# Transposing by DMA instead of on TensorE, with the DMA lists of SP and ACT reordered, in a fused cross-attention and quantized FFN kernel

## The chip, the cores and the metric

The kernel runs on one core of one Trainium2 chip. The metric is the device time of one execution in microseconds (us). A core has five engines with instruction lists of their own: TensorE (PE, matmuls and transposes by matmul), VectorE (DVE), ScalarE (ACT), GpSimd (POOL) and SyncE (SP, which here only issues DMAs). ACT issues DMAs too; SP and ACT have one DMA queue each, and both queues are served by the same 16 DMA engines. Each list runs strictly in order, and a semaphore wait in it holds everything behind it.

## What is computed

x and ctx are (16, 64, 256) float32: 16 batches, 64 rows, 256 columns. The attention has 8 heads of 8 rows; q is the layernorm of x, and ctx is both key and value.

```python
qk  = einsum('bhdq,bhdl->bhql', q, k) * 8**-0.5
ret = einsum('bhql,bhdl->bhdq', softmax(qk), v)
x   = x + gamma * ret
# the FFN, on a = layernorm(x); every bit_linear rounds its input rows to
# integers in -128..127 (scale: row maximum) and its weights to -1, 0, 1
h   = silu(bit_linear(a, w_gate)) * bit_linear(a, w_up)     # 256 -> 1024
h   = rms_norm(h, ln_weight)
out = x + bit_linear(h, w_down)                             # 1024 -> 256
```

## The kernel before

The 1024 rows are T = 8 tiles of 128 partitions (two batches each). A tile has 16 heads (BH), and the heads of all tiles are one stream of 128, numbered n. Time in the program is counted in half steps m: head n is at m = 2n, so a tile is 32 half steps. Every engine's list is written by a loop over m, and a table of numbers says at which m a piece of work stands: `tile_at(m, r)` gives the tile u with m = r + 32u. A larger number puts a piece later in that engine's list. All engines use the same m, so the numbers show who stands ahead of whom.

Each head has two score matmul pairs. A (psA, L433) gives scores with queries on partitions, from which DVE takes the negated row maximum (mneg, L736). B (psB, L447) gives the scores again, transposed, with the maximum already subtracted: three extra rows of q_stack hold the maxima as three bf16 parts, against rows of ones in k_stack. ACT takes the exponential (probs, L594), and a third matmul group (psO, L463, fp32) sums values and denominators for four heads at a time. B runs LAG = 14 heads behind A.

The maxima get there thus: for each half tile (8 heads) POOL splits them (m_parts), PE transposes them, ACT copies them to mt (L622), and SP moves 12 KB with a DMA (L398) from mt into the three rows of q_stack. This mt DMA stands at m = 20 + 16k. B of the first half of tile t waits for it at m = 29 + 32t.

The stacks: x (normalised, as xhat) and ctx are split into three bf16 parts (q_parts, k_parts), stored to scratch in HBM by six DMAs of 64 KB a tile (L301), and loaded back by six DMAs of 192 KB (L333, L341) into q_stack and k_stack, which have three buffers. SP_STORE = -26 and SP_LOAD = -20 place them: the loads of a tile are at m = 12 modulo 32. At the start SP also loads x and ctx of tiles 2 to 7 in two DMAs of 768 KB, and the three weights (1 MB each) in twelve DMAs spread over m = 12 to 33.

The FFN of a tile stands behind its attention, beside the heads of later tiles. DVE and POOL make the layernorm and its scale, ACT rounds (aq, L642), PE transposes aq in two 128x128 blocks (L520), ACT evicts to aT as bf16 (L648); PE multiplies by the gate and up weights in two halves (L535), ACT, DVE and POOL make h and weigh it (hw), DVE takes its row maximum (h_max, L834), ACT rounds (hq, L676), PE transposes eight blocks (L555), ACT evicts them to hT (L684), and PE multiplies by the down weight (L565). The weights are rounded once, in tile 1 (POOL L923, DVE L747), transposed by PE in twelve groups of four blocks (L498), and evicted by ACT and DVE in turn (L636, L755). Rounding adds and later subtracts 1.5 x 2^23. For the last tile some of this goes to DVE.

Of the kernel before, what the change touches and what calls it, by code (L numbers as in the profile page):

```python
# [5 lines left out]
ALU = mybir.AluOpType  # L29
# [5 lines left out]
P = 128  # L35
# [49 lines left out]
PE_WB, WB_STEP, WB_LAG = 56, 2, 0  # L85
POOL_INIT, DVE_STATS = 16, 14
# [28 lines left out]
def build(nc, x, ctx_in, gamma, w_gate, w_up, w_down, ln_weight, out):  # L115
# [7 lines left out]
    with ExitStack() as ctx:  # L123
# [48 lines left out]
        aq = sb("aq", [P, L])  # L172
        aT = sb("aT", [P, KC, P], BF16)
# [16 lines left out]
        hq = sb("hq", [P, HID])  # L190
        hT = sb("hT", [P, IC, P], BF16)
# [11 lines left out]
        wgT = sb("wgT", [P, 2, KC, HID], BF16)  # L203
        wdT = sb("wdT", [P, IC, L], BF16)
# [26 lines left out]
        s_stack = [sem(f"stack_loaded{i}") for i in range(NBUF)]  # L231
        s_a = sem("a_scores")
# [24 lines left out]
        s_aT = sem("aT_ready")  # L257
# [14 lines left out]
        s_hT = sem("hT_ready")  # L272
# [70 lines left out]

        def load_ones(eng, t):

            eng.dma_start(k_stack[STACK:STACK_M, t],
                          one_rows[:, :].unsqueeze(1).to_broadcast([PARTS, BH, L])).then_inc(s_ones[t], DMA)

        @block.sync
        def _(sp):  # L350
            def load_w(k, j):

                wide = w_sb[:, k, :].rearrange("p (c n) -> p c n", c=4)
                if k < 2:
                    rows = (w_gate, w_up)[k].rearrange("(j c p) n -> j p c n", c=2, p=P)[j]
                    sp.dma_start(wide[:, j, :].rearrange("p (c n) -> p c n", c=2), rows).then_inc(s_w[k], DMA)
                else:
                    half = slice(512 * (j % 2), 512 * (j % 2 + 1))
                    sp.dma_start(wide[:, j, :], w_down[P * (j // 2):P * (j // 2 + 1), half]).then_inc(s_w[k], DMA)

# [6 lines left out]
            load_q(sp, 0)  # L367
            sp.wait_ge(s_rows, 1)
            load_ones(sp, 0)
            sp.dma_start(x_sb[:, 2:T, :], x_rows[2:T].rearrange("g p l -> p g l")).then_inc(s_x[2], DMA)  # L370
            sp.dma_start(c_sb[:, 2:T, :], ctx_rows[2:T].rearrange("g p l -> p g l")).then_inc(s_c[2], DMA)
            for m in range(2 * FIRST, 2 * LAST):
                n = m // 2
                t = tile_at(m, SP_STORE)
# [19 lines left out]
                k = half_at(m, ACT_M)  # L394
                if k is not None:
                    t, half = divmod(k, 2)
                    sp.wait_ge(s_mtsb, k + 1)
# [610 lines left out]
```

## Time and profile before

| | us |
|---|---|
| median of 3 runs | 244.86 (244.29 to 246.13) |
| span of the profiled execution | 248.6 |
| PE busy | 178.4 (72%) |
| DVE busy | 151.6 (61%) |
| ACT busy | 140.9 (57%) |
| POOL busy | 107.3 (43%) |

The profile is of one execution; it lists busy time of each engine, the granted clock of TensorE in slices, and for every instruction what its engine waited for before it. Matmuls overlap, so a busy PE is not PE at its peak. A wait counts only where it stands on the path that sets the end.

### The profile page before, as it was taken

Reading aid. Unit: us, or ns where it says so; the run is one execution under the profiler, and the core shown is the slowest. Engines: PE = TensorE matmul, PEld = TensorE weight load, DVE = VectorE, ACT = ScalarE, POOL = GpSimd, SP = SyncE. Lnnn points to the kernel's source line nnn. Section 1 sums busy time; section 2 is a strip of 40 time slices with the busy share of each in tenths; the row PEclk is TensorE's granted clock in tenths of the full one; section 3 lists DMA queues with packets and bytes.
Section 4 is the critical chain, followed back from the end, with each engine's and each line's share of the span. In section 5 each row is a group of like instructions: output and inputs, shape, how many; then the busy total and the mean of one; then the engine's idle time right before and its main releaser. Section 6 shows DMA issues by size and latency. Waiting matters only on the chain.

```text
span 248.6 us, 4308 instructions
## 1 busy us (share of the span) xinstructions
PE 178.4 (72%) x1370; PEld 103.8 (42%) x1378; DVE 151.6 (61%) x282; ACT 140.9 (57%) x286; POOL 107.3 (43%) x282
## 2 busy tenths in 40 slices
PE   0006331972988958994999799589979998893793
PEld 0002111540666624662466366245745664441432
DVE  2105840563297974985666989736886769436273
ACT  4110000893466845973568599447856587975432
POOL 3630310406624544734652586436435226626240
PEclk9999999996599997997569999965995699999689
DMA  3599599348201450253026314601540000000000
GB/s 100 139 142 261 126 177 313 115 121 154 63 1 37 118 107 0 56 149 77 1 67 141 75 26 116 135 9 34 142 105 0 5 3 22 7 21 0 22 1 21
DMA packets 15871, 19.95 MB, mean 80 GB/s; under 512 B 2649, under 2 KB 14057, under 8 KB 14697
## 3 DMA queue, kind: packets, MB, share of 16 engines
q1 hardware_dynamic: 15321, 18.89, 31.8%
q10 hardware_dynamic: 528, 0.79, 1.4%
q8 instruction: 11, 0.18, 0.3%
q14 instruction: 11, 0.09, 0.1%
HBM read 15.20 MB, written 4.19 MB: 78 GB/s over the span
## 4 chain that ended last, share of the span: by engine, by line
PE 33%; DMA 14%; DVE 7%; issue 6%; ACT 6%; POOL 4%; SPq 3%; POOLq 0%; ACTq 0%; DVEq 0%
DMA q_stack<-mt 13%; PE psO L463 9%; PE psB L447 7%; PE psA L433 6%; PE psG L565 2%; PE psG L505 2%; ACT probs L594 2%; PE psG L555 2%; POOL hw L325 2%; DVE mneg L736 1%; SPq L333 1%; ACT o_sb L629 1%; SPq L341 1%; DVE wgT L755 1%; DVE w_sb L747 1%
## 5 line engine op out<-in xcount | busy, mean ns | idle before, releaser
L736 DVE TENSOR_REDUCE mneg<-psA 128x2 f32<-128x512 f32 x128 | 82.7, 680 | 46.5 <-PE psA L433 46.4
L594 ACT ACTIVATE probs<-psB 128x512 f32<-128x512 f32 x128 | 74.0, 597 | 39.8 <-PE psB L447 39.7
L433 PE MATMUL psA<-k_stack,q_stack 72*128 72x256 bf16 x256 | 57.9, 319 | 23.1 <-DMA q_stack<-q_scratch 20.7
L447 PE MATMUL psB<-q_stack,k_stack 75*128 75x256 bf16 x256 | 55.2, 303 | 23.8 <-DMA q_stack<-mt 22.0
L463 PE MATMUL psO<-probs,vt 128*32 128x256 f32 x512 | 41.6, 451 | 1.0 <-ACT probs L594 1.0
L433 PEld LDWEIGHTS psA<-k_stack,q_stack 72*128 72x128 bf16 x256 | 23.9, 108 | 43.3 <-issue 30.1
L447 PEld LDWEIGHTS psB<-q_stack,k_stack 75*128 75x128 bf16 x256 | 25.7, 108 | 37.2 <-DMA q_stack<-mt 23.8
L325 POOL TENSOR_TENSOR hw<-h,lnw 128x512 f32<-128x512 f32 x15 | 19.1, 1270 | 39.3 <-DVE h L826 28.0
L463 PEld LDWEIGHTS psO<-probs,vt 128*32 128x32 f32 x512 | 14.8, 121 | 16.9 <-issue 9.9
L815 DVE SCALAR_TENSOR_TENSOR gu<-th,psG 128x512 f32<-128x512 f32 x15 | 10.3, 688 | 9.7 <-ACT th L657 9.7
L657 ACT ACTIVATE th<-psG,tscale 128x512 f32<-128x512 f32 x15 | 10.3, 688 | 9.1 <-PE psG L535 9.0
L931 POOL CAST m_parts<-mneg 128x16 bf16<-128x16 f32 x16 | 3.7, 230 | 19.7 <-DVE mneg L736 12.4
L676 ACT ACTIVATE hq<-hw,h_sig 128x1024 f32<-128x1024 f32 (+1 forms) x8 | 8.7, 1091 | 5.3 <-POOL h_sig L984 2.8
L622 ACT ACTIVATE mt<-psU 48x128 bf16<-48x128 bf16 x16 | 4.3, 270 | 12.9 <-PE psU L479 12.9
L826 DVE TENSOR_TENSOR h<-psU,gu 128x512 f32<-128x512 f32 x15 | 10.4, 691 | 0.5
L834 DVE TENSOR_REDUCE h_max<-hw 128x1 f32<-128x1024 f32 x8 | 9.7, 1212 | 1.4 <-POOL hw L325 1.4
L694 ACT ACTIVATE vt<-psU 128x128 f32<-128x128 f32 x16 | 3.7, 298 | 12.0 <-PE psU L473 12.0
L505 PE MATMUL psG<-ident,o_sb 128*128 128x128 f32 x32 | 6.9, 354 | 4.2 <-ACT o_sb L629 3.3
L565 PE MATMUL psG<-wdT,hT 128*128 128x256 bf16 x64 | 9.1, 289 | 0.7 <-DVE hT L850 0.4
L535 PE MATMUL psU<-wgT,aT 128*128 128x512 bf16 x30 | 9.4, 395 | 0.1
L923 POOL TENSOR_SCALAR w_sb<-w_sb,winv 128x2048 f32<-128x2048 f32 x3 | 5.9, 1974 | 7.9 <-DVE whalf L743 7.9
L762 DVE RECIPROCAL rden<-psG 128x32 f32<-128x32 f32 x8 | 2.9, 357 | 9.4 <-PE psG L505 9.4
(129 smaller groups left out, 268.4 us busy)
## 6 DMA issues: line engine op xcount, KB each, us to landing
q_stack<-q_scratch SPq DMA_DIRECT2D x24, 192.0 KB
k_stack<-k_scratch SPq DMA_DIRECT2D x21, 192.0 KB
q_scratch<-q_parts SPq DMA_DIRECT2D x24, 64.0 KB, 2.1
k_scratch<-k_parts SPq DMA_DIRECT2D x21, 64.0 KB, 2.0
w_sb<-in_L_ffn_w_gate_dram SPq DMA_DIRECT2D x4, 256.0 KB, 8.0
w_sb<-in_L_ffn_w_up_dram SPq DMA_DIRECT2D x4, 256.0 KB, 7.5
w_sb<-in_L_ffn_w_down_dram SPq DMA_DIRECT2D x4, 256.0 KB, 4.1
out_dram<-y_sb SPq DMA_DIRECT2D x8, 128.0 KB, 4.2
```

The lines of the kernel that those rows point to most:

```text
L325: eng.tensor_tensor(hw[:, half], h[:, half], lnw[:, half], ALU.mult).then_inc(s_hw, 1)
L433: mm = pe.matmul(psA[n % A_BANKS][:, qt * L:(qt + 1) * L], q_stack[0:STACK, t % NBUF, bh, qt * P:(qt + 1) * P], k_stack[0:STACK, t % NBUF, ...
L447: mm = pe.matmul(psB[b % 2][:, lt * L:(lt + 1) * L], k_stack[:, t % NBUF, bh, lt * P:(lt + 1) * P], q_stack[:, t % NBUF, bh, :], start=Tru ...
L463: mm = pe.matmul(psO[32 * j:32 * (j + 1), half * L:(half + 1) * L], vt[:, t % 2, lt, half * GROUP + j, par, :], probs[:, (GROUP * g + j) % ...
L505: mm = pe.transpose(banks[BANK_OTR][:, k * P:(k + 1) * P], o_sb[:, k * P:(k + 1) * P], ident[:, :])
L565: mm = pe.matmul(banks[BANK_DOWN][:, 0:L], hT[:, ic, :], wdT[:, ic, :], start=(ic == 0), stop=(ic == IC - 1))
L594: act.activation(probs[:, b % RING, :], psB[b % 2][:, :], ACT.Exp, scale=SCALE).then_inc(s_exp, 1)
L657: act.activation(th[:, c, :], gate_up(u, c)[0][:, :], ACT.Tanh, scale=tscale[:, 0:1]).then_inc(s_th, 1)
L736: dve.tensor_reduce(mneg[:, k % MBUF, QT * (bh % HALF):QT * (bh % HALF + 1)], psA[n % A_BANKS][:, :].rearrange("p (q l) -> p q l", q=QT), ...
L815: dve.scalar_tensor_tensor(out=gu[:, c, :], in0=th[:, c, :], scalar=1.0, in1=gate_up(u, c)[0][:, :], op0=ALU.add, op1=ALU.mult).then_inc(s ...
L826: dve.tensor_tensor(h[:, c * 512:(c + 1) * 512], gate_up(u, c)[1][:, :], gu[:, c, :], ALU.mult).then_inc(s_h, 1)
L834: dve.tensor_reduce(h_max[:, :], hw[:, :], AX.X, ALU.max, apply_absolute_value=True).then_inc(s_hmax, 1)
```

## The change

1. SP's list: the mt DMA is written first at each m; the stores go to m = 21 modulo 32 (SP_STORE = -43) and the loads to m = 5 modulo 32 (SP_LOAD = -27). The making of the parts on ACT and POOL moves some 16 half steps ahead.
2. The stacks of tile 0 are loaded in halves of eight heads, and head 0 waits only for the first half. x and ctx of tiles 2 to 7, and each weight in one DMA, are issued by ACT, after all of tile 0's stacks landed.
3. aq is converted to bf16 by POOL (aq_b), hq likewise (hq_b), the rounded weights by DVE (wq_b), and `dma_start_transpose` on SP's queue writes aT, hT and the transposed weights. PE keeps these transposes for the last tile alone; the evictions go with them.
4. Gate, up, h, hq and down move some 5 to 9 half steps later in all lists.

Cut to what matters (the table of numbers in two lines, since its effect is shown below):

```diff
-SP_STORE, SP_LOAD, SP_OUT = -26, -20, 119
+SP_STORE, SP_LOAD, SP_AT, SP_HT, SP_OUT = -43, -27, 82, 115, 128
...
+        def load_first(eng, k, half):
+            heads = slice(half * HALF, (half + 1) * HALF)
+            done = (s_first, s_stack[0])[half]
+            for c in range(PARTS):
+                rows = slice(REP * c, REP * (c + 1))
+                if k == 0:
+                    eng.dma_start(k_stack[rows, 0, heads, :].rearrange("p b l -> p (b l)"),
+                                  k_scratch[0, :, c, heads].rearrange("d b l -> d (b l)").unsqueeze(1)
+                                  .to_broadcast([DH, PARTS, HALF * L])).then_inc(done, DMA)
+                else:
+                    eng.dma_start(q_stack[rows, 0, heads, :].rearrange("p b l -> p (b l)"),
+                                  q_scratch[0, :, :, heads].rearrange("d c b l -> (d c) (b l)")).then_inc(done, DMA)
...
+                k, off = divmod(m - SP_WT, WQ_STEP)
+                if off == 0 and 0 <= k < 3:
+                    sp.wait_ge(s_wb, k + 1)
+                    dst = wgT[:, k].rearrange("p i k q -> p (i k) q") if k < 2 else wdT[:, :, :, :].rearrange("p h i q -> p (h i) q")
+                    sp.dma_start_transpose(dst, wq_b[:, k, :]).then_inc(s_wT, DMA)
+                u = tile_at(m, SP_AT)
+                if u is not None and u < T - 1:
+                    sp.wait_ge(s_aqb, u + 1)
+                    if u:
+                        sp.wait_ge(s_u, 2 * u)
+                    sp.dma_start_transpose(aT[:, :, :], aq_b[:, :]).then_inc(s_aTd, DMA)
+                u = tile_at(m, SP_HT)
+                if u is not None and u < T - 1:
+                    sp.wait_ge(s_hqb, u + 1)
+                    if u:
+                        sp.wait_ge(s_y, u)
+                    sp.dma_start_transpose(hT[:, :, :], hq_b[:, :]).then_inc(s_hTd, DMA)
...
+                if m in ACT_BULK:
+                    j = ACT_BULK.index(m)
+                    if j == 0:
+                        act.wait_ge(s_first, 2 * PARTS * DMA)
+                        act.wait_ge(s_stack[0], 2 * PARTS * DMA)
+                        act.dma_start(x_sb[:, 2:T, :], x_rows[2:T].rearrange("g p l -> p g l")).then_inc(s_x[2], DMA)
...
+                    dve.wait_ge(s_wq, k + 1)
+                    dve.tensor_scalar(wq_b[:, k, :], w_sb[:, k, :], ROUND, None, ALU.subtract).then_inc(s_wb, 1)
...
+                u = tile_at(m, POOL_HB)
+                if u is not None and u < T - 1:
+                    pool.wait_ge(s_hq, u + 1)
+                    if u:
+                        pool.wait_ge(s_hTd, DMA * u)
+                    pool.tensor_scalar(hq_b[:, :], hq[:, :], -ROUND, 0.0, ALU.add, ALU.add).then_inc(s_hqb, 1)
```

SP's list in a middle tile, before. x2 means that the row stands twice; L398 is the mt DMA, L403 the store of a finished tile.

```order
L398 DMA q_stack<-mt 3x16x128 [waits max_rows_copied]
L301 DMA k_scratch<-k_parts 16x8x256 [waits first_part]
...
L301 DMA q_scratch<-q_parts 16x8x256 [waits third_part]
L333 DMA k_stack<-k_scratch 24x1x4096 [waits k_part0_stored0,b_scores]
...
L341 DMA q_stack<-q_scratch 24x4096 x2
L398 DMA q_stack<-mt 3x16x128 [waits max_rows_copied]
L403 DMA out_dram<-y_sb 128x256 [waits out_made]
```

The same place after the change:

```order
L363 DMA q_stack<-mt 3x16x128 [waits max_rows_copied]
L314 DMA k_stack<-k_scratch 24x1x4096 [waits k_part0_stored0,b_scores]
...
L322 DMA q_stack<-q_scratch 24x4096 x2
L394 DMA_TRANSPOSE aT<-aq_b 128x2x128 [waits up_done,a_as_bf16]
L400 DMA_TRANSPOSE hT<-hq_b 128x8x128 [waits down_done,h_as_bf16]
L363 DMA q_stack<-mt 3x16x128 [waits max_rows_copied]
L282 DMA k_scratch<-k_parts 16x8x256 [waits first_part]
```

The loads stood close ahead of the first half's mt; now they stand close behind the other half's, and two transposing DMAs stand between them and the first half's mt.

PE's list in a middle tile after the change, where the transposed data are wanted (L555 is down, L526 gate and up, L450 B):

```order
L555 MATMUL psG<-wdT,hT 128x256 [waits hT_landed,x1_made]
L555 MATMUL psG<-wdT,hT 128x256 x7
L450 MATMUL psB<-q_stack,k_stack 128x256 [waits exps]
L450 MATMUL psB<-q_stack,k_stack 128x256
L526 MATMUL psG<-wgT,aT 128x512 [waits out_made,aT_landed]
L526 MATMUL psG<-wgT,aT 128x512
L526 MATMUL psU<-wgT,aT 128x512 [waits max_rows_copied]
L526 MATMUL psU<-wgT,aT 128x512
L436 MATMUL psA<-k_stack,q_stack 128x256 [waits row_max]
L436 MATMUL psA<-k_stack,q_stack 128x256
L450 MATMUL psB<-q_stack,k_stack 128x256 [waits exps,max_rows_loaded0]
```

Down of the tile before (m = 26), gate (27) and B's wait for mt (29) now stand within three half steps.

## Rows read from the trace of the kernel before

**Rows 1.** The page: the granted clock in 40 slices.

```profile
PEclk9999999996599997997569999965995699999689
```

**Rows 2.** Waits: whole run, then about 162.5 and 86 (total, times, longest).

```profile
PE psB L447 <- DMA q_stack<-mt: 22.0, 6, 8.7
...
PE psB L447 <- DMA q_stack<-mt: 3.8, 1, 3.8
...
PE psB L447 <- DMA q_stack<-mt: 3.2, 1, 3.2
```

**Rows 3.** Timeline of SP's queue: start, duration, line, what was issued.

```profile
62.75 14.71 SPq L398 DMA_DIRECT2D q_stack<-mt  x2
...
82.27 2.19 SPq L333 DMA_DIRECT2D k_stack<-k_scratch  x3
...
86.56 14.66 SPq L398 DMA_DIRECT2D q_stack<-mt  x2
...
192.56 11.49 SPq L398 DMA_DIRECT2D q_stack<-mt  x2
```

**Rows 4.** The chain that ended last, about the mt of tile 2.

```profile
86.56 7.27 DMA q_stack<-mt
93.87 0.39 PE psB L447 x2
```

**Rows 5.** Stretches: length, busy of PE, PEld, DVE, ACT, POOL; clock, DMA.

```profile
66.00:86.00 20.00, 18.00 (x166) 13.04 (x164) 16.97 (x31) 13.78 (x30) 7.88 (x23) 0.96 0.15 39
...
140.70:154.70 14.00, 13.26 (x129) 8.69 (x131) 12.41 (x25) 12.53 (x29) 10.10 (x31) 1.00 0.21 56
154.70:162.50 7.80, 4.06 (x35) 1.98 (x34) 5.18 (x9) 3.35 (x6) 3.08 (x3) 1.00 0.59 127
162.50:180.10 17.60, 17.30 (x128) 10.60 (x130) 11.40 (x22) 12.73 (x29) 9.23 (x30) 0.71 0.23 63
...
185.70:203.00 17.30, 17.05 (x127) 10.77 (x128) 11.94 (x24) 11.32 (x23) 7.46 (x27) 0.70 0.01 2
```

**Rows 6.** DMA: 79 to 81 (stores), 85 to 87 (loads), a store's landing.

```profile
q1 hardware_dynamic: 444, 0.20, 39.5%
...
q1 hardware_dynamic: 69, 0.41, 73.6%
...
k_scratch<-k_parts SPq DMA_DIRECT2D x21, 64.0 KB, 2.0
```

**Rows 7.** Groups by line: busy, mean ns of one, idle before.

```profile
L923 POOL TENSOR_SCALAR w_sb<-w_sb,winv 128x2048 f32<-128x2048 f32 x3 | 5.9, 1974 | 7.9 <-DVE whalf L743 7.9
...
L498 PE MATMUL psG<-ident,w_sb 128*128 128x128 f32 x24 | 4.1, 299 | 0.7 <-DVE on L770 0.7
...
L747 DVE TENSOR_SCALAR w_sb<-w_sb 128x2048 f32<-128x2048 f32 x3 | 3.7, 1221 | 1.5 <-POOL w_sb L923 1.5
```

**Rows 8.** Start: timeline of SP, PE and DVE; x's load from the page.

```profile
9.60 1.50 SPq L341 DMA_DIRECT2D q_stack<-q_scratch  x3
...
20.70 4.37 PE L433 MATMUL psA<-k_stack,q_stack 72*128 72x256 bf16 x16 [20.70 <-DMA q_stack<-q_scratch]
...
25.52 2.04 DVE L725 BATCH_NORM_STATS2 stats<-x_sb 128x6 f32<-128x256 f32 x6
...
32.64 0.78 SPq L398 DMA_DIRECT2D q_stack<-mt  x1
...
42.59 0.61 PE L447 MATMUL psB<-q_stack,k_stack 75*128 75x256 bf16 x2 [8.70 <-DMA q_stack<-mt]
...
x_sb<-in_x_dram SPq DMA_DIRECT2D x1, 768.0 KB, 11.1
```

**Rows 9.** Timeline of the end: h_inv and hq of tile 6, then tile 7.

```profile
227.96 0.32 POOL L979 TENSOR_SCALAR h_inv<-h_max,cr 128x1 f32<-128x1 f32 x1 [0.18 <-POOL cr L974]
...
229.23 1.15 ACT L676 ACTIVATE hq<-hw,h_sig 128x1024 f32<-128x1024 f32 x1 [2.62 <-POOL h_sig L984]
...
231.46 0.42 DVE L804 TENSOR_REDUCE a_max<-xn 128x1 f32<-128x256 f32 x1
...
235.04 0.63 PE L535 MATMUL psG<-wgT,aT 128*128 128x512 bf16 x1 [0.88 <-ACT aT L648]
```

More of the change, by code:

```diff
@@ L172, in build @@
         aq = sb("aq", [P, L])
+        aq_b = sb("aq_b", [P, L], BF16)
         aT = sb("aT", [P, KC, P], BF16)
@@ L350, in _ @@
         def _(sp):
[L351 to L359, printed above, removed]
             for t in range(2):
@@ L393, in _ @@
                     sp.dma_start(gam[:, :], gamma.partition_broadcast(P)).then_inc(s_lnw, DMA)
[L394 to L397, printed above, removed]
-                    sp.dma_start(q_stack[STACK:STACK_M, t % NBUF, half * HALF:(half + 1) * HALF, :]
-                                 .rearrange("c b (q l) -> c (b q) l", q=QT), mt[:, k % 2, :]).then_inc(s_mrow[half], DMA)
+                k, off = divmod(m - SP_WT, WQ_STEP)
[15 more added lines that the diff above has]
+                    sp.dma_start_transpose(hT[:, :, :], hq_b[:, :]).then_inc(s_hTd, DMA)
                 u = tile_at(m, SP_OUT)
@@ L420, in keep_clock @@
                 for _ in range(count):
-                    pe.matmul(psB[0][:, :], aT[:, 0, :], wgT[:, 0, 0, 0:512], start=True, stop=True)
+                    pe.matmul(psB[0][:, :], aT[:, 0, :], wgT[:, 0, 0:4, 0, :], start=True, stop=True)
             pe.wait_ge(s_ident, 2)
@@ L427, in _ @@
                     t, i, bh = unit(n)
-                    if i == 0:
+                    if n == 0:
+                        pe.wait_ge(s_first, 2 * PARTS * DMA)
+                    elif i == (0 if t else HALF):
                         pe.wait_ge(s_stack[t % NBUF], 2 * PARTS * DMA * (t // NBUF + 1))
@@ L515, in _ @@
                 u = tile_at(m, PE_ATR)
-                if u is not None:
-                    take(BANK_ATR, s_aT, u + 1)
+                if u == T - 1:
+                    take(BANK_ATR, s_aT, 1)
                     pe.wait_ge(s_aq, u + 1)
@@ L547, in _ @@
                     u = tile_at(m, r)
-                    if u is not None:
-                        last = (u, c) == (T - 1, 0)
-                        pe.wait_ge(*((s_hq, u + 1) if not last else (s_hq_last, 1)))
+                    if u == T - 1:
+                        pe.wait_ge(*((s_hq_last, 1), (s_hq, T))[c])
                         bank = banks[(BANK_HTR0, BANK_HTR1)[c]]
-                        take((BANK_HTR0, BANK_HTR1)[c], *((s_hT, min(2 * u + c + 1, 2 * T - 1)) if not last else (s_hT_last, 1)))
+                        take((BANK_HTR0, BANK_HTR1)[c], (s_hT_last, s_hT)[c], 1)
                         for j in range(4):
@@ L585, in _ @@
             act.wait_ge(s_p3, 2)
-            load_k(act, 0)
+            for c in range(PARTS):
+                act.wait_ge(s_kst[c][0], DMA)
+            load_first(act, 0, 0)
+            load_first(act, 0, 1)
             for m in range(2 * FIRST, 2 * LAST):
```

150 lines of the change are left out of this document (71 added, 79 removed).

## The prediction

> **What bounds the kernel now.** I read the page first, then the waits, then the stretches between them. The page gives a span of 248.6 us for the profiled execution; the median of the plain runs is 244.86 us, 1.5% less, so the sum is made against 248.6 and scaled by 0.985 at the end. Its clock line [rows 1] shows full clock (2.4 GHz) broken by four dips of about 12 us each to near the lower level (1.2 GHz). The waits [rows 2] name one culprit: the B matmuls (psB, L447) wait 22.0 us in six waits for the 12 KB DMA that puts the negated row maxima (mt) into q_stack. The longest, 8.7 us, is at the start; the other five share 13.3 us, and a typical bad one is 3.8 us.
>
> SP's rows [rows 3] show why. The six loads of the next tile's stacks are issued from 82.27 on, and mt only at 86.56, behind them on the same queue; it lands 7.27 us later [rows 4]. From the first load to that landing are 11.6 us; the same distance in the other tiles is near 11.
>
> The stretches [rows 5] give the price. From 140.7 to 162.5, a tile of 21.8 us, the clock was full and PE was busy 13.26 + 4.06 = 17.3 us. Take off the 3.8 us that psB waited and a tile needs 18.0 us. In the stretches from 162.5 and 185.7 the same 128 or so matmuls took 17.30 and 17.05 us at granted clocks of 0.71 and 0.70, against 13.26 at 1.00: each bad tile pays some 4 us for the clock beside the wait, after PE had stood. mt was issued at 86.56 for tile 2 and at about 203.3 for tile 7 [rows 3], so a tile takes 23.3 us now.
>
> **The change, part by part.** *SP's list.* The loads now follow at once behind the mt of one half tile (step 5 of 32), and the next mt is at step 20. B needs mt at step 29: 24 half steps after the loads begin, 13.5 us in a tile of 18 us, against 8.4 us now (82.27 to PE's arrival at 90.7, which is 93.87 [rows 4] less its wait of 3.2 [rows 2]). The loads and mt together took 11.6. Alone this would remove all five waits, and with them the reason for the dips.
>
> But two transposing DMAs, aT and hT, now stand between the loads and mt, in the same queue, with two consumers of their own: down (PE step 26) and gate (step 27). Their price is the open one. Nothing in this trace transposes by DMA. I count in blocks of 128x128 bf16 (32 KB): aT is 2, hT 8, each weight 16. The nearest row by size of piece: in 79 to 81 us, 444 small packets took 39.5% of 16 engines over 2 us, 28 ns each [rows 6]. A block is 128 runs of 256 B, shorter than these packets of some 450 B; I take 26 ns each, which over 16 engines makes **0.21 us**. Below that, a block as cheap as bytes moved by the stack loads (0.41 MB in 2 us while they ran [rows 6]) is 0.16 us. Above it, a block that needs an issue of its own costs like the stack loads' issues, 2.19 us for three, or 0.73 [rows 3]. I take 0.21, the row nearest in shape; 0.16 and 0.73 stay as ends.
>
> At 0.21, aT and hT add 2.1 us to the 11: hT is there 13.1 us after the loads began, down wants it at 21 half steps or 11.8 us, so PE waits about 1.3 us, and gate and mt are then ready. Call it 1 us a tile.
>
> The Trainium skill speaks against the change: VectorE: DVE Perf Modes, The three transpose paths, gives 1309 ns for a 128x128 bf16 block by DMA and 390 ns on TensorE. By it the sum below would end near 333 us. Another page of the Trainium skill, Advanced Engine Details and Errata, X-Bar Transpose (TRN2), has these DMAs nearly as fast as plain ones (350 to 400 GB/s); by that, an estimate of 0.09 us a block, the result would be near 206. No row here shows either.
>
> *Work leaving PE.* aT's and hT's transposes in seven tiles: ten blocks each, like those of the weights near 0.17 us (4.1 us of 24 [rows 7]), less at full clock, about 1.3 us of PE a tile, and three evictions less on ACT. PE is then at 16.0, but DVE is not relieved: it was busy 12.41 + 5.18 = 17.6 us in the tile from 140.7 [rows 5], which this change leaves. So the tile stays at 18.0, now bound by DVE, and 18.0 + 1 = 19.0 against 23.3: five tiles give **21.5 us**. The conversions on POOL (1 us for hq, half of 1974 ns for 2048 columns, and 0.5 for aq [rows 7]) hide under POOL's idle third; without it they would lengthen the chain to hT.
>
> *Weights.* 48 PE transposes of 0.17 us leave: 8 us off the tile of 23.8 us from 62.75 to 86.56 [rows 3, 7]. DVE loses its six evictions and pays three conversions of 2048 columns, near 1.2 us each as its own pass over a weight is [rows 7], some 3.7 for what was 4: no difference. It was busy 16.97 of the 20 us from 66 to 86 [rows 5], so no more than its 3.0 us of idle time can go: **3 us**. The three weight DMAs, 48 blocks or 10 us, have 20 half steps (13 us) before B wants the next mt; covered, barely.
>
> *Start.* A starts at 20.70, 11.1 us after the q loads were issued at 9.60 [rows 8]. With half stacks loaded first, A starts at 14 to 18. But A head 7's maximum waits on DVE for statistics of x of six tiles, and that load is issued later than now: by ACT, after all stacks landed, at about 18. It takes between 4.5 us (0.77 MB at the 200 GB/s of [rows 6]) and the 11.1 it took [rows 8], so it lands at 22.5 to 29. From statistics to issue of mt 7.1 us pass now (25.52 to 32.64) [rows 8]; mt then finds the loads of tile 1 done. B starts at 32 to 39 against 42.59; I take 34, a gain of **8.6 us**. Until 62.75 nothing else moves.
>
> *Tail.* Tile 6 was helped by PE transposes; now its down stands directly ahead of tile 7's gate in PE's list, and ACT's hq of tile 6 ahead of tile 7's aq. Now a_max of tile 7 starts at 231.46, its gate at 235.04 [rows 9], and hq of tile 6 is over before. In the new order DVE takes tile 6's h_max (1.2 us) only after that a_max, then follow POOL's chain 1.3 (227.96 to 229.23), hq 1.15 [rows 9], the conversion 1.0, the DMA 3.7 (a 64 KB store lands in 2.0 [rows 6], and 8 blocks are 1.7), down 1.0: about 9.4 us after a_max where gate now comes after 3.6. **+6 us.**
>
> Sum: 21.5 + 3 + 8.6 - 6 = 27.1; 248.6 - 27.1 = 221.5, by 0.985 **218 us**.
>
> **One number carries the risk.** Let b be the us per block. A tile's stall is 10b - 1, five times; the weights cost 48b less the 10 that fit; the tail 8b. Together the change of the span is -27.1 + 106(b - 0.21). It is zero at b = 0.47.
>
> **Rivals.** *A, slower: the transposes clog SP's queue.* The place is SP's queue between the stack loads and mt; it decides from b = 0.47 on. At b = 0.6 the stall is 5 us a tile, the weights alone hold mt some 19 us, and the time is (248.6 - 27.1 + 41.3) x 0.985 = 259 us. For it: 0.73 as the upper bound; hT would hold mt every tile. Against: the small-packet row. 0.13. The 1309 ns of the Trainium skill (VectorE: DVE Perf Modes) would be a case of this rival.
>
> *B, the wait moves.* b is near 0.3, or the loads end later because the conversions and waits of SP's in-order list hold them. PE stands 2 to 3 us a tile, at hT rather than at mt, and the clock dips stay in some tiles: a tile of 22 instead of 19. 218 + 15 = 233 us, or 228 if only the stands stay (106 x 0.09 above the forecast). For it: all three consumers lie within 3 half steps, and the slack is under 2 us. 0.17.
>
> *C, better than forecast.* b at 0.16 or below and B starting at 32: the stall (5 us) and 2 us of the start go, tiles of 17.7: 218 - 8.5 = 209 us or less. 0.12.
>
> *D, gain and loss meet* (b from 0.44 to 0.49): within 1%, 0.03.
>
> **Numbers.** The forecast case (211 to 225 us) has 0.55. The range is 207 to 234: it leaves out A, D and a thin end of C. A difference of 1% is about what can be told from none. Faster: forecast, B and C, 0.84; within 1%, 0.03; slower, A, 0.13.
>
> **What would show it.** Right: no wait of psB for mt over 1 us after the first; waits of down for hT near 1 us; a granted clock above 0.95 from 80 us on; mt issues 19 us apart per tile; B starting by 36 us; a longer gap between the last psO and the last gate, near 16 us. Wrong: DMA transposes landing over 4 us after issue with an idle queue (A), a tile of 22 with dips (B), x landing after 29 us (the start's gain gone). If the first gate matmul waits long for the weights, the 48 blocks were mispriced.

## The result, and the profile after

The changed kernel takes **319.64 us** (median of 4 runs, 316.89 to 320.8) against 245.5 us of the kernel before, a ratio of 1.301 (95% interval 1.291 to 1.310). The forecast was 218 us, the range 207 to 234. Medians here are of all executions and ratios of the faster ones alone (an execution more than 1.5% above its kernel's fastest is left out of them), and the profile of the kernel before, with its span of 248.6 us, is of an execution some 2 us slower than any of the four behind its median.

The page of the changed kernel, its span, busy times and the granted clock in 40 slices (compare [rows 1]):

```profile
span 315.1 us, 4050 instructions
...
PE 181.0 (57%) x1260; PEld 88.3 (28%) x1260; DVE 156.8 (50%) x279; ACT 129.5 (41%) x259; POOL 142.2 (45%) x296
...
PEclk9999999857599967995799589958995975576579
```

PE has 118 transposes fewer (48 of weights, 14 of aq, 56 of hq) and was busy longer: the clock now dips in nearly every tile, where before it dipped four times. POOL has 35 us more. The waits (total, times, longest), the last for comparison with [rows 2]:

```profile
DVE mneg L730 <- PE psA L436: 90.7, 40, 9.3
...
POOL hw L306 <- DVE h L815: 58.2, 8, 10.3
...
POOL rstd L927 <- DVE mv L780: 31.8, 8, 4.7
...
ACT hq L672 <- POOL h_sig L985: 26.4, 7, 7.8
...
ACT k_parts L605 <- DMA c_sb<-in_ctx_dram: 21.2, 1, 21.2
...
PE psG L555 <- DMA hT<-hq_b: 11.2, 2, 6.1
...
PE psB L450 <- DMA q_stack<-mt: 4.9, 1, 4.9
```

PE's wait for mt is gone but for the first (4.9, where the six took 22.0), as forecast, and hT makes PE wait twice only. What grew are waits of POOL, ACT and DVE for one another. SP's queue in a tile, and the transposes' median time from issue to landing (compare [rows 3]):

```profile
149.93 0.82 SPq L363 DMA_DIRECT2D q_stack<-mt  x1
...
165.32 2.14 SPq L314 DMA_DIRECT2D k_stack<-k_scratch  x3
167.51 1.27 SPq L322 DMA_DIRECT2D q_stack<-q_scratch  x3
177.89 1.22 SPq L394 DMA_TRANSPOSE aT<-aq_b  x1
179.20 1.25 SPq L400 DMA_TRANSPOSE hT<-hq_b  x1
```

```profile
aT<-aq_b SPq DMA_TRANSPOSE x7, 2.4
hT<-hq_b SPq DMA_TRANSPOSE x7, 3.1
...
wgT<-wq_b SPq DMA_TRANSPOSE x2, 4.3
wdT<-wq_b SPq DMA_TRANSPOSE x1, 4.5
```

The DMAs are not slow: 2, 8 and 16 blocks land in 2.4, 3.1 and 4.3 us. But aT is issued 9 us after the loads, since SP stood waiting for aq_b. The whole tile, and two stretches in it (columns as in [rows 5]):

```profile
149.90:180.90 31.00, 19.20 (x156) 9.76 (x154) 17.32 (x30) 14.98 (x33) 16.93 (x35) 0.83 0.28 68
170.00:175.00 5.00, 1.49 (x10) 0.74 (x10) 3.04 (x5) 2.82 (x5) 4.41 (x12) 0.85 0.57 123
175.00:180.90 5.90, 1.17 (x5) 0.53 (x6) 0.00 (x0) 2.02 (x7) 5.48 (x9) 0.50 0.15 32
```

In these 10.9 us PE is busy 2.7 us, DVE not at all in the second half, and POOL 9.9 us. Its list there (start, duration, instruction, and in brackets the idle time before it and what ended that):

```profile
165.56 0.19 POOL L927 TENSOR_SCALAR rstd<-mv 128x1 f32<-128x1 f32 x1 [4.12 <-DVE mv L780]
...
166.36 1.27 POOL L306 TENSOR_TENSOR hw<-h,lnw 128x512 f32<-128x512 f32 x1
...
170.50 0.19 POOL L985 TENSOR_TENSOR h_sig<-h_rec,cr 128x1 f32<-128x1 f32 x1
...
173.18 3.65 POOL L961 TENSOR_SCALAR hq_b<-hq 128x1024 bf16<-128x1024 f32 x1
176.79 1.07 POOL L955 TENSOR_SCALAR aq_b<-aq 128x256 bf16<-128x256 f32 x1
177.86 0.55 POOL L892 TENSOR_SCALAR xhat<-x_sb,rstd,shift 128x256 f32<-128x256 f32 x1
```

15 us without a gap over 0.3 us: POOL first waited 4.12 us for mv with h ready behind it, then came all of h's pieces, then hq_b at 3.65 us (the prediction had 1), then aq_b, then xhat and m_parts. ACT stood 4.89 us for that xhat with exponentials behind it in its list, and PE stood 6.21 us for the exponentials.

**Where the 66.5 us between the two profiled spans are** (by the issue of the first mt of each tile; before, by [rows 3, 8]): the start +5.4 (38.0 against 32.6), tile 0 to 1 -1.8, tile 1 to 2 +0.7, the five tiles to tile 7 +33.9 (30.1 us each against 23.3), from there to the end +28.3 (73.6 against 45.3), which holds most of one more slow tile and the tail.

### The profile page after: what moved, and what is told of

It reads as the page before. It is cut to its first block and busy times, and to the rows that moved or that the text cites. A ratio compares the mean times of both kernels' runs of the same rounds, so it can differ in the third digit from the quotient of the medians.

```text
span 315.1 us, 4050 instructions
## 1 busy us (share of the span) xinstructions
PE 181.0 (57%) x1260; PEld 88.3 (28%) x1260; DVE 156.8 (50%) x279; ACT 129.5 (41%) x259; POOL 142.2 (45%) x296
## 5 line engine op out<-in xcount | busy, mean ns | idle before, releaser
L450 PE MATMUL psB<-q_stack,k_stack 75*128 75x256 bf16 x256 | 59.2, 323 | 41.1 <-ACT probs L587 35.4
L436 PE MATMUL psA<-k_stack,q_stack 72*128 72x256 bf16 x256 | 59.2, 326 | 25.8 <-DMA q_stack<-q_scratch 16.6
L466 PE MATMUL psO<-probs,vt 128*32 128x256 f32 x512 | 46.4, 494 | 0.0
L450 PEld LDWEIGHTS psB<-q_stack,k_stack 75*128 75x128 bf16 x256 | 24.8, 112 | 60.1 <-ACT probs L587 45.1
L961 POOL TENSOR_SCALAR hq_b<-hq 128x1024 bf16<-128x1024 f32 x7 | 25.5, 3648 | 0.6
L847 DVE SCALAR_TENSOR_TENSOR y_sb<-psG,yscale,x 128x256 f32<-128x256 f32 x8 | 3.9, 484 | 32.7 <-PE psG L555 32.7
L482 PE MATMUL psU<-ident_b,m_parts 128*48 128x128 bf16 x16 | 4.3, 266 | 24.4 <-POOL m_parts L923 15.1
L555 PE MATMUL psG<-wdT,hT 128*128 128x256 bf16 x64 | 10.6, 321 | 11.6 <-DMA hT<-hq_b 11.2
L526 PE MATMUL psG<-wgT,aT 128*128 128x512 bf16 x30 | 10.2, 427 | 10.8 <-DVE gu L804 7.6
L927 POOL TENSOR_SCALAR rstd<-mv 128x1 f32<-128x1 f32 x8 | 1.5, 190 | 31.8 <-DVE mv L780 31.8
L605 ACT ACTIVATE k_parts<-c_sb 128x256 bf16<-128x256 f32 x7 | 2.9, 413 | 27.0 <-DMA c_sb<-in_ctx_dram 21.2
L555 PEld LDWEIGHTS psG<-wdT,hT 128*128 128x128 bf16 x64 | 7.2, 115 | 14.5 <-issue 12.0
```

The source lines that it names most:

```text
L436: mm = pe.matmul(psA[n % A_BANKS][:, qt * L:(qt + 1) * L], q_stack[0:STACK, t % NBUF, bh, qt * P:(qt + 1) * P], k_stack[0:STACK, t % NBUF, ...
L450: mm = pe.matmul(psB[b % 2][:, lt * L:(lt + 1) * L], k_stack[:, t % NBUF, bh, lt * P:(lt + 1) * P], q_stack[:, t % NBUF, bh, :], start=Tru ...
L466: mm = pe.matmul(psO[32 * j:32 * (j + 1), half * L:(half + 1) * L], vt[:, t % 2, lt, half * GROUP + j, par, :], probs[:, (GROUP * g + j) % ...
L526: mm = pe.matmul(bank[:, :], aT[:, kc, :], wgT[:, w, 4 * c:4 * (c + 1), kc, :], start=(kc == 0), stop=(kc == KC - 1))
L555: mm = pe.matmul(banks[BANK_DOWN][:, 0:L], hT[:, ic, :], wdT[:, :, ic, :], start=(ic == 0), stop=(ic == IC - 1))
L961: pool.tensor_scalar(hq_b[:, :], hq[:, :], -ROUND, 0.0, ALU.add, ALU.add).then_inc(s_hqb, 1)
```

## The experiments

Two theories to start with. **The ring:** the tile is a ring of dependent work through in-order lists, and the conversions and the late FFN pieces made that ring longer than PE's work. **The queue:** SP's new order or the transposing DMAs in it hold the tile up. Letters of theories are those of each expectation. A short diff shows the main numbers of the table that differ; the matching pieces of the other engines move with them. Differences in us are of medians. Runs whose labels begin with the same letter were measured together; between such groups the kernel before itself moved by some us, so there the difference of two ratios (0.01 is 2.5 us) is the surer one.

### The SP order, and the late places

*x4: the kernel before, with part 1 of the change alone.*

```diff
-ACT_QK1, ACT_QK2 = -31, -25   POOL_XHAT, POOL_QK1, POOL_QK3 = -29, -26, -19   SP_STORE, SP_LOAD = -26, -20
+ACT_QK1, ACT_QK2 = -48, -41   POOL_XHAT, POOL_QK1, POOL_QK3 = -46, -42, -35   SP_STORE, SP_LOAD = -43, -27
+ the mt DMA written first at each m
```

> The kernel before with only the making, storing and loading of the stacks moved ahead and mt first in SP's list; FFN places, PE's transposes and the start are as before. The prediction's term for SP's list: the five waits of psB for mt (13.3 us) and part of the clock dips go, 220 to 235. If the waits only move to another engine: 240 to 247.

Measured 226.33 us, ratio 0.935 (0.925 to 0.944). Its clock line and one tile:

```profile
PEclk9999999999559999999999999999999999999599
105.25:124.06 18.81, 17.48 (x163) 10.75 (x164) 16.53 (x31) 16.20 (x35) 12.23 (x33) 1.00 0.40 98
```

A tile of 18.8 us at full clock with PE busy 17.5: the mechanism of this term of the prediction was right, and this one piece beats both kernels, by 16 us (14 to 18) in the ratio to the kernel before. It is the base for what follows.

*x3: x4 with all FFN places of the change (PE's transposes kept).*

```diff
-PE_G0, PE_G1, PE_HTR0, PE_HTR1, PE_DOWN = 86, 88, 105, 108, 113      POOL_HW0, POOL_HW1, POOL_CR, POOL_H = 97, 100, 100, 101
+PE_G0, PE_G1, PE_HTR0, PE_HTR1, PE_DOWN = 91, 93, 110, 113, 122      POOL_HW0, POOL_HW1, POOL_CR, POOL_H = 100, 104, 105, 107
```

> The kernel before with the changed kernel's places for all pieces and its order of SP's list, but no transposing DMAs, no conversions, and the start as before: PE transposes and ACT evicts as before. Theory L (the places alone cost the time): over 290. Theory P: the loads no longer stand ahead of mt, so it is near the kernel before or better, 230 to 250; the tail is still longer by some 5 us since tile 6's down stands ahead of tile 7's gate.

295.44 us, ratio 1.221 (1.204 to 1.237): **the late places alone, without one transposing DMA, cost 69 us** (Theory L). The queue is out as the main cause.

*y3: x3 with h's pieces ahead of the next tile's rstd on POOL* (HW0, HW1, CR, H = 100, 101, 102, 102; rstd stands at 103; on DVE h_max goes from 105 to 100).

> As x3_late_ffn (no transposing DMAs, PE transposes; 295 us) with the same h pieces put ahead. Theory R: near x4_sp_order_only (226) plus a longer tail, 228 to 245. Rival S: over 270, since hq, transposes and down stay at their late steps.

275.51 us, ratio 1.117 (1.106 to 1.128). POOL's order was 20 us of the 69 (26 by the ratios); 49 stay, which is Rival S.

*z2: x4 with hq, its transposes, down and out late (in the last tile alone its gate part is late too); z3: x4 with gate, tanh and h late* (h's pieces as in y3; hq, its transposes and down 2 steps later).

```diff
z2  -ACT_HQ, PE_HTR0, PE_HTR1, PE_DOWN = 101, 105, 108, 113    +ACT_HQ, PE_HTR0, PE_HTR1, PE_DOWN = 108, 110, 113, 122
z3  -PE_G0, PE_G1, ACT_HQ, PE_DOWN = 86, 88, 101, 113          +PE_G0, PE_G1, ACT_HQ, PE_DOWN = 91, 93, 103, 115
```

> The kernel before with the new SP order (226.3 us by itself) and only the down part late: hq 108, its PE transposes 110 and 113, down and out 122, the gate part at the places of before (86 to 101; in the last tile alone 5 steps later, since its down has to stand behind). With gate and down both late and h's POOL pieces ahead of the next rstd it was 275.5. Theory K, late pieces cost only where gate (step 27, 29) and down (26) stand together in the two shared banks psG and psU, one eviction behind the other: here down 26 stands 2 steps behind G1 (24) and 6 ahead of the O transposes, so little: 226 to 240. Theory L, down's place alone (its bank is handed on to the O transposes, its late end holds back y_sb and h of the next tile): 260 or more.

> The same base with only the gate part late: G0, G1 91 and 93, tanh 91, 92, g*u 93 to 95, h's pieces on POOL 100 to 102, hq 103, transposes 107 and 110, down 115. Theory K as above: gate 27, 29 stand 10 steps behind down (19) and 3 ahead of the O transposes (32): 226 to 240. Theory G, gate's own place costs (its second half at 29 and h*u at 31 stand right ahead of the O transposes at 32, so psG and psU are handed on one behind the other there, and with them the next tile's x1, xn): 260 or more, and the trace then has PE waiting for gu or th of DVE and ACT ahead of its next B.

250.5 us (ratio 1.025, 0.992 to 1.058) and 251.09 us (1.031, 1.022 to 1.041). All theories missed: 24.2 and 24.8 us over x4, and together (y3) 49.2 (by the ratios 22, 24 and 45). The two add up, so a crowd of gate and down in the shared banks (Theory K) does not explain them, and neither place is harmless. One tile of z2, one of y3, one of z3:

```profile
130.00:154.42 24.42, 20.46 (x164) 11.19 (x165) 16.80 (x30) 16.57 (x35) 12.20 (x33) 0.90 0.30 71
111.65:139.62 27.97, 22.08 (x166) 11.76 (x165) 16.81 (x30) 16.53 (x35) 12.27 (x33) 0.87 0.25 63
130.49:152.63 22.14, 18.01 (x165) 10.67 (x164) 16.59 (x31) 15.98 (x35) 12.27 (x33) 1.00 0.33 80
```

DVE, ACT and POOL are as busy as in x4. In z2 and y3 PE does the same work in 3 to 4.6 us more, at a lower clock, and the rest is standing; in z3's tile the clock is full and nearly all of the 3.3 us is standing. No single wait is long: PE's in the tile of z2 are 1.3 us and less. But PE's waits of the whole run of z2 show where they are:

```profile
PE psG L557 <- ACT hq L678: 6.3, 7, 1.2
...
PE psU L522 <- ACT hT L686: 4.9, 7, 1.8
PE psU L557 <- ACT vt L696: 4.3, 5, 1.3
```

With 3.7 us of down's waits for gu these are 19.2 us, where x4 has 1.9 us for hq, 1.7 for vt at this bank, and none of the others: 15.6 of the 23.4 us between the two spans. Three of the four are waits for the piece that empties a shared PSUM bank. In psU (hT and vt, 9.2 us) the transposes of ctx, hq and aq stand at steps 15, 17 and 18 in z2 (hq's at 12 in x4), and in psG (gu) down stands 2 steps behind gate. So the hand-over of banks goes with what down's place costs, and the one at psU is a part that the changed kernel does not have, since its PE transposes neither hq nor aq but in the last tile. In z3 it is mostly waits for hq (9.7 us) and of gate for gu (8.4), where x4 has 1.9 and none. No run took the banks apart.

### The conversions

*x1: the changed kernel, with DVE in POOL's place for aq_b and hq_b.*

```diff
-pool.tensor_scalar(hq_b[:, :], hq[:, :], -ROUND, 0.0, ALU.add, ALU.add)
+dve.tensor_scalar(hq_b[:, :], hq[:, :], ROUND, None, ALU.subtract)
```

> The changed kernel with one difference: the two conversions to bf16 (aq_b, hq_b) are made by DVE instead of POOL, at the same steps. Theory P (POOL's slow conversions, 3.65 + 1.07 us a tile, stand in the loop through POOL, ACT and PE): six or seven tiles lose at least 4.7 us each, so 320 falls to 285 or less; if the stall was amplified through ACT's wait for xhat, to 265. Theory L (the crowded, later places of the FFN's pieces cost the time, whoever converts): over 305. DVE should need about 0.65 us for 1024 columns, by its 1.23 us for 2048.

293.46 us, ratio 1.213 (1.203 to 1.222): 26 us come back (22 by the ratios), less than Theory P wanted and more than Theory L allowed.

*x2: the changed kernel, xhat 6 steps earlier on POOL, out of the block* (POOL_XHAT -52 for -46, POOL_INIT 11 for 16).

> The changed kernel with xhat of POOL (and the statistics it needs) placed ahead of the two conversions instead of behind them. ACT's q_parts waits 4.9 us a tile for xhat with exponentials behind it. Theory Q (the loss comes through what is queued behind the conversions on POOL, above all xhat): 5 to 7 us less in each of five tiles, 290 or less. Theory P in its plain form (the chain to m_parts and mt is as long as before): at most 2 us a tile less, 305 to 318.

318.96 us, ratio 1.316 (1.290 to 1.343): no change. ACT's 16.2 us of waits for POOL's xhat are gone, but PE now waits 28.1 us for m_parts, which stand behind the same conversions, instead of 15.1.

*y4: a probe, x4 with twelve POOL instructions behind everything else; its total means nothing.*

> x4_sp_order_only with twelve operations on POOL alone at its end, on 128x1024 float32: two forms of the conversion by an immediate (bf16 and float32 out), two by a column scalar, a plain cast and a subtraction of two tensors. If the type of the result is what makes hq_b slow (3.65 us, 3.6 ns a column, against 0.96 ns in the rounding of the weights), the bf16 forms take over 3 us and the float32 forms near 1; if it is the immediates, the forms with a column scalar take near 1 whatever the type; if it is DVE working beside it, all are near 1 here.

```profile
222.91 3.65 POOL L995 TENSOR_SCALAR pr_b<-hq 128x1024 bf16<-128x1024 f32 x1 [4.47 <-DVE y_sb L864]
226.65 3.63 POOL L996 TENSOR_SCALAR pr_f<-hq 128x1024 f32<-128x1024 f32 x1
230.37 1.12 POOL L997 TENSOR_SCALAR pr_g<-hq,a_inv 128x1024 f32<-128x1024 f32 x1
231.59 1.12 POOL L998 TENSOR_SCALAR pr_c<-hq,a_inv 128x1024 bf16<-128x1024 f32 x1
```

The first two have two immediates, the last two a column scalar and one immediate. The first form costs 3.3 times as much, whatever the output type, on a POOL with nothing beside it. The operations differ too (add, add against mult, add); two immediates with mult, add were not tried, so the scalars and the operations stay unseparated.

*z1: the changed kernel, the conversions by column scalar.*

```diff
-pool.tensor_scalar(hq_b[:, :], hq[:, :], -ROUND, 0.0, ALU.add, ALU.add)
+pool.tensor_scalar(hq_b[:, :], hq[:, :], ones[:, 0:1], -ROUND, ALU.mult, ALU.add)
```

> The changed kernel with one thing else: POOL subtracts ROUND in its two conversions by a column scalar (a column of ones, multiplied, then the immediate added) in place of two immediates. Theory F, the form of the instruction is what costs: the probe took 1.12 us for 128x1024 so, and 3.65 us with two immediates, so seven hq_b save 2.5 us each and seven aq_b about 0.8 us each, 23 us in all on POOL's block that the tile waits for: 297 us (292 to 302), about what DVE as converter gave (293). Rival, that POOL has any conversion at all in its block is the cost, whatever it takes: over 310 us.

300.36 us, ratio 1.230 (1.217 to 1.244). The form of the two conversions is 19 us of the changed kernel (17 by the ratios), as Theory F had it.

*y1: the changed kernel, h's pieces ahead of rstd; y2: the same and DVE converting.*

> The changed kernel with h's chain put ahead again: on POOL hw, cr and h_sig at steps 100 to 102 (before rstd of the next tile at 71 + 32 = 103), on DVE h_max at 100; everything else as changed, POOL still converts. Theory R (the changed table puts POOL's rstd of the next tile ahead of the second half of hw, so h's chain waits for the next tile's layernorm, and ACT's hq with exponentials behind it waits 26 us in all for h_sig): that wait falls under 6 us and the time by the placement's part, 40 us or more: 250 to 280. Rival S (it is the later hq, transposes and down that cost): 305 or more.

> As y1_h_first, with the conversions on DVE as in x1_dve_conv. If R and the slow conversions are the two causes: a tile near 19 to 20 us and 225 to 240 in all. If the transposing DMAs ahead of mt still cost: 10b - 1 = 1 to 3 us more a tile, up to 250.

307.13 us (1.251, 1.231 to 1.272) and 278.03 us (1.124, 1.105 to 1.144): 12 to 15 us for POOL's order here, where it was 20 without the DMAs. y1 ends with Rival S, and y2 lies 28 us above the most that its expectation allowed.

### The transposes by themselves

*z4: column scalar, and every piece nearly as early as before* (gate 88 and 90 for 86 and 88, hq 103 for 101, down 115 for 113).

```diff
-PE_G0, PE_G1, PE_DOWN = 91, 93, 122   POOL_HW0, POOL_HW1, POOL_CR, POOL_H, POOL_HB = 100, 104, 105, 107, 111   SP_HT, SP_OUT = 115, 128
+PE_G0, PE_G1, PE_DOWN = 88, 90, 115   POOL_HW0, POOL_HW1, POOL_CR, POOL_H, POOL_HB = 98, 100, 101, 102, 104    SP_HT, SP_OUT = 105, 121
```

> The changed kernel with the conversions on POOL by column scalar and every FFN piece as near to its place of before as the transposing DMAs allow: aq_b 80, aT by SP at 82, gate 88 and 90, h's pieces 98 to 102, hq 103, hq_b 104, hT by SP at 105, down and out 115. Start and tail as in the changed kernel. If places and form are all that went wrong and the DMA transposes themselves cost about what they were priced at, the tiles come to 19 to 21 us and the time to 226 to 245 us (start and tail keep about 14 us over). If the transposes by DMA or the two more waits of SP's list cost by themselves, the tiles stay at 25 us or more and the time at 265 or more.

281.16 us, ratio 1.152 (1.136 to 1.168): the second case. hT landed 7.3 us after its issue and PE waited 23.5 us for it, since its issue now came just behind the six stack loads.

*v1: z4 with the loads behind hT* (SP_LOAD -22 for -27).

> The run with early places and the column-scalar conversion (281 us, tiles of 29 us) with one number changed: the six stack loads of the next tile come behind hT's transpose on SP (SP_LOAD -22 in place of -27). Theory Q, hT lands late (7 to 8.6 us, against 3.1 in the changed kernel) because the rings are full of 1.1 MB of stack loads issued just ahead of it, and PE waits 5.4 us a tile for it with all else behind: hT lands in 3 to 4 us, the wait on hT goes to about 1 us, tiles come to 21 to 24 us, 235 to 250 us in all. Rival, the transposes are slow by themselves once they are in use beside other traffic, or the chain through SP is: tiles stay over 27 us, 270 us or more.

281.82 us, ratio 1.156 (1.149 to 1.163). Landing times:

```profile
aT<-aq_b SPq DMA_TRANSPOSE x7, 7.2
hT<-hq_b SPq DMA_TRANSPOSE x7, 3.1
```

hT is quick, and now aT is the late one (PE waits 20.4 us for it): the price changed hands. The time is the rival's.

*v2: v1 with the whole start of before.*

> The same kernel with the whole start of before (stacks loaded whole, bulk loads and weights' loads issued by SP, weights in twelve pieces), the transposes by DMA kept. The first mt was issued at 32.7 us with before's start and at 38.0 and 37.2 with the new one, while the step from it to the second was 29.6 and 29.0: so the start costs about 5 us, and this run is 4 to 6 us below the one beside it. If the clogged start only hides a wait that comes anyway (weights, ctx), the two are equal within 2 us.

276.35 us, ratio 1.130 (1.116 to 1.144): the new start costs 5.5 us.

*w1: v2 with the loads behind both* (SP_LOAD -12); *w2: v2 with the loads issued by ACT.*

> The run with early places, column-scalar conversion and before's start (276.4 us) with one number changed: the six stack loads of the next tile at SP_LOAD -12, behind hT's and aT's transposes and the row-max DMA. Theory Q (a transpose issued behind the stack loads lands 7 us after its issue, alone 2.4 to 3.1, and PE then waits 5.5 us a tile): both waits go, and unless the loads, now 12 steps ahead of their first use, come too late themselves, the tile comes to 20 to 22 us, 230 to 246 us in all. Rival, the loads become the late ones and A waits for its stack 3 us or more a tile: 250 to 262 us. Rival, the transposes cost by themselves: no change, over 268 us.

> The same base (276.4 us, stack loads at -22 between the two transposes) with the loads issued by ACT, on its own queue. Theory Q1, it is the order within SP's queue: aT lands in 2.4 to 3 us again in spite of the loads, 240 to 255 us (ACT loses 3.4 us of issue a tile, about 45% busy otherwise). Theory Q2, the sixteen DMA engines are shared and the transposes' small packets stand beside the loads' there whatever the queue: aT still lands in 5 us or more and the time stays at 268 to 280 us.

283.47 us (1.162, 1.153 to 1.171) and 302.12 us (1.226, 1.196 to 1.256). Waits of w1, then landings of w2:

```profile
PE psA L445 <- DMA q_stack<-q_scratch: 54.5, 8, 20.5
```

```profile
aT<-aq_b SPq DMA_TRANSPOSE x7, 9.6
hT<-hq_b SPq DMA_TRANSPOSE x7, 10.0
```

In w1 both transposes land in 2.3 and 3.1 us, but A now waits for its stack, 34 us beside the 20.5 of the start: the first rival's mechanism, at more than its 262 us. In w2 another queue made both transposes slower, so the order within one queue (Q1) is out. That fits Q2, DMA engines that both queues share, though the time lies above its 280 us and ACT's list, which issued the loads, was disturbed too.

*v3: x4 with the weights alone by DMA.*

> The kernel before with the new SP order (226.3 us by itself) and the weights alone transposed by DMA, rounded weights made bfloat16 by DVE (3 x 1.23 us), no PE transposes and no evictions of them. In the prediction this was worth 3 us. The weights' pieces stand in tile 1 (14.1 + 10.1 us from the mt at 62.3 to the one at 86.4, against 18.8 in later tiles), so at most about 5 us can come back: 221 to 226 us. Rival, the three transposes (512 KB each, 4.3 us to landing) stand on SP between mt and the stack loads and make the first B of that tile wait: 227 to 232 us.

226.75 us, ratio 0.929 (0.918 to 0.940): not to be told from x4. In the weights' tile (the first mt of tile 1 to that of tile 2) PE is busy 18.7 us for 22.0, and the tile takes 23.5 us for 24.2.

*u1: v3 with hT by DMA too, aT by PE; places of before (down at 114 for 113), loads behind hT.*

> The new SP order, before's start and the places of before (gate 86 and 88, down 114), weights and hT transposed by DMA, aT by PE and ACT again, hq_b by column scalar on POOL, the stack loads behind hT's transpose. Theory R, there is room for one: hT lands in 3.1 us with nothing late behind it, the stack loads have 22 steps, nothing of aT stands behind them. Then the tile is PE's own, 17.5 us busy of 18.8 without the eight transposes of hq (1.3 us of PE in each tile) at best, and the time is that of the run with only the weights by DMA (226.8) or a little less: 220 to 232 us. Theory S, each transpose by DMA costs several us a tile by itself (SP waits in order for hq_b, POOL has 1.1 us more, packets of 2 bytes by row load the engines): about half of the 50 us that both cost, 245 to 260 us.

251.89 us (247.2 to 253.0; before 246.9 beside it), 25 over v3: Theory S's number, while hT itself landed in 3.1 us and PE never waited for it. Of S's reasons, POOL's 1.1 us stands in the rows below. Packets of 2 bytes do not stand in the trace: u1 has 7391 packets more than v3 for its 56 blocks, 132 for the 32 KB of one, so a packet is near 250 bytes. POOL's list in u1, and PE's one wait that grew:

```profile
119.44 0.19 POOL L966 TENSOR_TENSOR h_sig<-h_rec,cr 128x1 f32<-128x1 f32 x1
...
120.91 1.12 POOL L942 TENSOR_SCALAR hq_b<-hq,ones 128x1024 bf16<-128x1024 f32 x1 [1.13 <-ACT hq L659]
122.11 0.19 POOL L914 TENSOR_SCALAR rstd<-mv 128x1 f32<-128x1 f32 x1
...
127.73 0.44 PE L511 MATMUL psU<-ident,aq 128*128 128x128 f32 x2 [2.25 <-ACT vt L675]
```

and the same place of x4:

```profile
115.28 0.19 POOL L984 TENSOR_TENSOR h_sig<-h_rec,cr 128x1 f32<-128x1 f32 x1
...
116.73 0.19 POOL L938 TENSOR_SCALAR rstd<-mv 128x1 f32<-128x1 f32 x1 [1.12 <-DVE mv L791]
```

From h_sig to the next tile's rstd 1.45 us pass in x4, where POOL even waits for mv, and 2.67 in u1, where it waits 1.13 us for hq and converts 1.12. What hangs on rstd (a_inv, xhat, vt, the transpose of aq) comes that much later, and PE stands 2.25 us. The whole tile of u1:

```profile
130.81:154.79 23.98, 20.43 (x157) 10.53 (x156) 16.53 (x30) 15.64 (x33) 13.35 (x34) 0.86 0.36 85
```

It is 5.2 us longer than x4's, and 2.95 of that is PE busy at a clock of 0.86, with six matmul records fewer in the tile. **In this tile a stand of some 2 us was paid twice: once standing, once at the lower clock beside it.** That the one brought the other is read from their standing side by side; no run changed the stand alone.

## Why the prediction was wrong, step by step

- *SP's list, 21.5 us:* the mechanism was right, in a kernel that keeps everything else: x4's tiles take 18.5 us from tile 2 to tile 7 (18.8 for a full one) where 18.0 was worked out, and 24 us less than before lie between the two profiled spans. Over the whole run it is 16 us (14 to 18) by the ratio; the 23.3 us a tile was read from the one execution of 248.6 us.
- *b, us per block, 0.21:* the number that was to carry the risk was right as time of the DMA engines: from 123.4 to 125.2 us of u1, 1011 packets, nearly all of them hT's, took 90.0% of 16 engines, 26 ns each, and 132 of them are 0.21 us. In landing time it was on the safe side: hT's six blocks more than aT cost 0.7 us (0.12 a block), and the weights' eight more 1.2 (0.15). What the term lacked is the 2.2 us of each landing that do not depend on size. The Trainium skill's figure (VectorE: DVE Perf Modes, The three transpose paths), 1309 ns a block, would by an estimate be 10.5 us for hT where the trace has 3.1 for the whole DMA: the measurement decides against it as a price per block. *Rival A* gave the right sign by the wrong mechanism. It comes true only where a transpose is in flight with the stack loads: 7.2 to 10.0 us (v1, z4, w2). *Rival B* had SP's in-order list right (it stood for aq_b until 9 us after the loads) and priced it at 15 us.
- *"The conversions hide under POOL's idle third":* **the step that failed first.** The size was wrong (3.65 us, not 1.0: halving the 1974 ns of [rows 7] took over the time of an instruction with a column scalar for one with two immediates), and so was the reasoning: idle share is no cover for an instruction that stands in order between h_sig and the next rstd. 19 us by z1, 26 by x1. How much of u1's 25 us it costs even at 1.12 us was not tried.
- *The late places:* **the step with the largest miss.** The prediction listed them and charged them 6 us in the tail and nothing in a tile (its 1 us a tile was for hT's landing). Alone they cost 69 us (x3): 25 for gate, 24 for down, 20 for h's pieces behind rstd. The tile was taken as the larger of two engines' busy times, 18.0. It is also a ring: gate, h, POOL's chain, rstd of the next tile, its aq, its gate. That fits h behind rstd and gate. Down alone (z2) leaves POOL's pieces where x4 has them and costs as much, in waits at psU and for hq, so the ring as named is not all of it.
- *Work leaving PE, 3 us for the weights, tiles to 18.0 by DVE:* worth nothing that shows (v3: +0.4 us on x4 in the medians, -0.006 in the ratio; 0.7 us in the weights' tile). PE was busy 17.5 of 18.8 us of x4's other tiles; that work leaving it there would only make more idle time is argued, not shown by a run without other costs.
- *Start, -8.6:* it came to +5.4 (v2 and v1: 5.5). A did start earlier, at 16.6, but ACT issued the bulk loads: its issues of the up and down weights took 8.4 and 6.6 us, and its next work stood until ctx had landed (16.5 us after its issue), 21 us of idle time:

```profile
19.23 0.44 ACTq L593 DMA_DIRECT2D x_sb<-in_x_dram  x1
...
20.89 8.37 ACTq L598 DMA_DIRECT2D w_sb<-in_L_ffn_w_up_dram  x1
29.28 6.55 ACTq L598 DMA_DIRECT2D w_sb<-in_L_ffn_w_down_dram  x1
...
36.29 0.42 ACT L605 ACTIVATE k_parts<-c_sb 128x256 bf16<-128x256 f32 x1 [21.25 <-DMA c_sb<-in_ctx_dram]
```

  The prediction counted when x would land, and that came out (24.2, in its 22.5 to 29, though 0.77 MB at 200 GB/s are 3.9 us and not its 4.5). It did not count ctx, nor what ACT could do meanwhile.
- *Tail, +6:* the mechanism was right, the size not: from a_max of tile 7 to its gate (301.52) were 14.3 us, not 9.4, and 11.7 of them to down's first matmul, where the sum has 8.4 (compare [rows 9]). The conversion is 2.6 us of the excess:

```profile
287.25 0.42 DVE L793 TENSOR_REDUCE a_max<-xn 128x1 f32<-128x256 f32 x1
...
292.13 3.65 POOL L961 TENSOR_SCALAR hq_b<-hq 128x1024 bf16<-128x1024 f32 x1
295.81 1.23 SPq L400 DMA_TRANSPOSE hT<-hq_b  x1
...
298.98 1.23 PE L555 MATMUL psG<-wdT,hT 128*128 128x256 bf16 x5 [6.08 <-DMA hT<-hq_b]
```

**How the parts meet.** In ratios to the kernel before, turned into us of its 245.5: SP's order -16; gate and down late +45; h behind rstd +26; both DMAs, the column-scalar conversions and the new start together only +2 (x3 to z1); the two immediates +17: 319.6 with rounding. At early places the same two DMAs and conversions cost some 50 (v2 over x4; 48 by the ratios), and that holds what v2's places, 2 steps later than x4's, cost by themselves. So late places and transposes by DMA are not two prices to be added. One reading is that the places buy the latency of the DMA route; another is that x3 pays at psU for transposes of hq which the changed kernel does not make. The runs do not part them.

**What stays open.** Why each late place costs 3 us a tile is read from the ring, the waits and their adding up, not isolated: no run lengthened the ring by a known time, and none gave hq's transposes a bank of their own. How the 25 us of u1 divide between POOL's conversion and the transpose was not tried (DVE converting there would tell). Why a second queue made the transposes slower than the first is open too; ACT's own list was disturbed in that run.

## What to carry to other kernels

When tiles overlap in in-order lists, work out the ring (the dependent path from one tile's piece to the next tile's same piece) beside each engine's busy time, and charge every piece that is moved or inserted on it in full, per tile. An engine's idle share hides nothing that stands on that ring (the conversions: 17 to 26 us, with POOL busy 45% of the span), and work taken off an engine may be worth nothing (v3). Where pieces share a buffer, here the bank psU, look at who fills it next. Try the parts of a change alone: here one part was worth 16 us, and the rest cost some 90.

## What the runs showed of the hardware that was not expected

- POOL, 128x1024 fp32: add, add with two immediates 3.65 us, mult, add with a column scalar and an immediate 1.12 us, for fp32 and bf16 output alike (y4). For 128x256 the changed kernel had 1.07 us, z4 0.48.
- A transposing DMA of 64 KB landed in 2.4 us and one of 256 KB in 3.1 without loads just ahead of it, in 7.2 (v1) and 7.3 (z4) issued just behind 1.15 MB of stack loads, in 9.6 and 10.0 beside them from another queue (w2). Its packets took 26 ns of an engine each, as the small packets of [rows 6] take 28.
- An issue of a DMA, 0.44 to 0.57 us otherwise, held ACT for 8.4 us when 2.5 MB had been issued on its queue in the 1.7 us before.
- DVE's xn took 1.09 to 1.20 us in the middle tiles of the changed kernel and of x3, with POOL's hw beside it, and 0.41 in those of x4.
